# Selective scan on one core: residual added by TensorE, x1 copied by ScalarE, nine products on GpSimd, fourth step size in chunk 4

## What is computed

```python
x = x + s6(layernorm(x))                      # x1
def s6(x):
    xp = einsum('bld,ed->ble', x, x_proj_w)   # 64 ranks, 16 B, 16 C
    delta = softplus(einsum('blr,dr->bld', xp[..., :64], dt_proj_w) + dt_proj_b)
    deltaA = exp(einsum('bld,dn->bldn', delta, A))
    deltaB_u = einsum('bld,bln,bld->bldn', delta, B, x)
    h = deltaA[t] * h + deltaB_u[t]           # over the 1024 rows, for each (d, n)
    y = einsum('bdn,bn->bd', h, C[t])
    return y + x * D
x = x + chosen_tokens(layernorm(x))           # router, attention, MLP
```

## Time and profile before

| | |
|---|---|
| time, median of 3 runs | 4675.12 us (4675.03 to 4675.64) |
| the profiled execution's own time | 4677.7 us |
| its span in the profile | 4675.8 us |
| busy share of the span: DVE, POOL, PE, ACT | 83%, 76%, 59%, 59% |
| scan stage, about | 75 to 3640 us |
| chosen tokens, about | 3640 to 4676 us |

### The profile page before, as it was taken

How to read it: one execution, slowest core, us unless ns; L and a number is a source line. 1 busy time by engine, 2 the same in 40 slices (tenths; PEclk the granted TensorE clock), 3 DMA queues, 4 the chain that set the end, 5 groups by cost and what they waited for, 6 DMA issues and landing times. The chain is left out here.

```text
span 4675.8 us, 57243 instructions
## 1 busy us (share of the span) xinstructions
PE 2747.1 (59%) x15526; PEld 1014.5 (22%) x15526; DVE 3888.9 (83%) x3306; ACT 2753.9 (59%) x4103; POOL 3546.3 (76%) x1796
## 2 busy tenths in 40 slices
PE   3555454546454546454555545454644179999997
PEld 1111111111111111111111111111111145555553
DVE  3999999999999999999999999999999654445552
ACT  5676767767667676776767676776764322223221
POOL 4999999999999999999999999999998100000000
PEclk7556565656565656565555656565655589999999
DMA  4354545363545445454545454545353300000000
GB/s 102 95 132 113 137 110 152 93 160 84 157 99 148 111 132 134 113 137 108 136 110 132 113 137 109 151 95 159 84 141 69 153 16 21 18 23 18 18 18 7
DMA packets 198208, 472.72 MB, mean 101 GB/s; under 512 B 60688, under 2 KB 61200, under 8 KB 197088
## 3 DMA queue, kind: packets, MB, share of 16 engines
q1 hardware_dynamic: 177136, 452.11, 38.1%
q0 software_dynamic: 20736, 16.88, 1.4%
HBM read 126.83 MB, written 73.43 MB: 43 GB/s over the span
## 5 line engine op out<-in xcount | busy, mean ns | idle before, releaser
L879 POOL TENSOR_TENSOR ch<-hid,cmat 128x1024 f32<-128x1024 f32 x1024 | 2391.4, 2363 | 100.7 <-DVE hid L733 83.8
L733 DVE TENSOR_TENSOR_SCAN hid<-decay,inp 128x1024 f32<-128x1024 f32 x1024 | 2288.2, 2271 | 96.5 <-ACT decay L600 95.2
L600 ACT ACTIVATE decay<-delr,a_neg 128x1024 f32<-128x1024 f32 x1024 | 1136.4, 1112 | 807.4 <-DVE hid L733 797.3
L399 PE MATMUL ps_y<-ch,nsum 128*32 128x256 f32 x8192 | 997.7, 587 | 861.5 <-POOL ch L879 857.0
L722 DVE TENSOR_TENSOR inp<-dx,bmat 128x1024 f32<-128x1024 f32 x832 | 958.4, 1209 | 63.0 <-ACT dx L608 63.0
L399 PEld LDWEIGHTS ps_y<-ch,nsum 128*32 128x32 f32 x8192 | 249.2, 143 | 1597.1 <-POOL ch L879 1369.5
L408 PE MATMUL ps_y<-ident,ysb 128*128 128x128 f32 x512 | 169.4, 432 | 677.2 <-ACT ysb L615 660.6
L844 POOL TENSOR_TENSOR inp<-dxr,bmat 128x1024 f32<-128x1024 f32 x192 | 454.6, 2368 | 0.0
L394 PE MATMUL ps_y<-xhT,dskip 128*32 128x256 f32 x2048 | 272.2, 624 | 143.0 <-DVE xr L743 143.0
L1132 POOL DMA_INDIRECT out_rows<-row,idx_out x16 | 41.2, 2573 | 401.9 <-issue 220.9
L408 PEld LDWEIGHTS ps_y<-ident,ysb 128*128 128x128 f32 x512 | 71.7, 197 | 905.3 <-ACT ysb L615 861.7
(11 more groups left out here) (165 smaller groups left out, 3825.1 us busy)
## 6 DMA issues: line engine op xcount, KB each, us to landing
dxr<-dxT SPq DMA_DIRECT2D x1024, 128.0 KB, 2.4
delr<-delT SPq DMA_DIRECT2D x1024, 128.0 KB, 2.4
xr<-in_x SPq DMA_DIRECT2D x32, 1024.0 KB, 5.5
bmat<-b_and_c SPq DMA_DIRECT2D x256, 128.0 KB, 3.4
cmat<-b_and_c SPq DMA_DIRECT2D x256, 128.0 KB, 2.9
x_rows<-xr SPq DMA_DIRECT2D x16, 2048.0 KB, 7.7
out_rows<-xr SPq DMA_DIRECT2D x32, 1024.0 KB, 4.4
w<-in_w SPq DMA_DIRECT2D x2, 4096.0 KB, 23.8
```

Of the source, the lines that this page charges most:

```text
L399: last = pe.matmul(ps_y[q * CH:(q + 1) * CH, 0:2 * P], nsum[:], ch[:, g, q * 2 * P:(q + 1) * 2 * P], start=False, stop=(g == GROUPS - 1))
L600: nc.scalar.activation(decay[:, g % 2, :], delr[:, c % 2, :], ACT.Exp, scale=a_neg[:, i:i + 1])\
L733: nc.vector.tensor_tensor_scan(hid[:, g, :], decay[:, g % 2, :], inp[:, g, :], 0.0, ALU.mult, ALU.add).then_inc(hid_ready, 1)
L879: nc.gpsimd.tensor_tensor(ch[:, g, :], hid[:, g, :], cmat[:, g, :], ALU.mult).then_inc(ch_ready, 1)
```

## The change

TensorE now adds the residual: after each of the two products that turn y, it adds x itself by a product with the identity, into the same place in PSUM, so that PSUM holds x1. A new `copy_x1` on ScalarE copies that to `xr`, behind the exp of the next chunk's group 0, and it alone now raises `y_added`. VectorE's `add_y` is gone. `OWN_AT` loses chunks 1, 4 and 7, so GpSimd makes nine input products a batch. The fourth step size moves from chunk 1 to chunk 4, its second half on TensorE behind group 1 of that chunk, and its four GpSimd steps to chunks 5 to 7. It therefore comes after the router's use of `aux`, and waits for it. `SUMS1` and `SUMS2` are spread anew over chunks 5 and 6 and over chunks 0 to 2.

```diff
-YADD = 2
-SUMS1 = {(5, 1): range(0, 2), (5, 2): range(2, 4), (5, 3): range(4, 8), (6, 0): range(8, 10), (6, 1): range(10, 12), (6, 2): range(12, 14), (6, 3): range(14, 17)}
+SUMS1 = {(5, 2): range(0, 2), (5, 3): range(2, 5), (6, 0): range(5, 8), (6, 1): range(8, 11), (6, 2): range(11, 14), (6, 3): range(14, 17)}
-SUMS2 = {(0, 1): range(0, 2), (0, 2): range(2, 4), (0, 3): range(4, 8), (1, 0): range(8, 10), (1, 1): range(10, 12), (1, 2): range(12, 14), (1, 3): range(14, 17)}
+SUMS2 = {(0, 2): range(0, 3), (0, 3): range(3, 6), (1, 0): range(6, 8), (1, 1): range(8, 11), (1, 2): range(11, 13), (1, 3): range(13, 15), (2, 0): range(15, 17)}
-Z3 = 1
+Z3 = 4
-         (3, 2): (0, 3, 0), (4, 0): (0, 3, 1), (4, 2): (0, 3, 2), (5, 0): (0, 3, 3)}
+         (5, 2): (0, 3, 0), (6, 0): (0, 3, 1), (6, 2): (0, 3, 2), (7, 1): (0, 3, 3)}
-OWN_AT = (1, 3, 4, 5, 6, 7, 8, 9, 10, 11, 12, 13)
+OWN_AT = (3, 5, 6, 8, 9, 10, 11, 12, 13)
...
             def turn_xhat(b, t):
-                if t == 0 and has(b, 2):
-                    pe.wait_ge(router_sum, b * TC - TC)
...
             def step_size(b, k, h):
+                if k == 3 and h == 0 and has(b, 1):
+                    pe.wait_ge(router_sum, b * TC)
...
-            def turn_y(b, c):
+            def turn_y(b, par, c):
                 pe.wait_ge(ysb_ready, b * CHUNKS + c + 1)
                 for t in range(2):
-                    last = pe.transpose(ps_y[:, (2 + t) * P:(3 + t) * P], ysb[:, t * P:(t + 1) * P], ident[:])
+                    out_t = ps_y[:, (2 + t) * P:(3 + t) * P]
+                    x_t = xr[:, par, :, c * CH:(c + 1) * CH].rearrange("p (q t) d -> p t q d", t=2)[:, t]
+                    pe.matmul(out_t, ysb[:, t * P:(t + 1) * P], ident[:], start=True, stop=False)
+                    last = pe.matmul(out_t.rearrange("p (q d) -> p q d", q=4), ident[:], x_t, start=False, stop=True)
                 last.then_inc(yt_ready, 1)
...
+                        for h, at in ((0, (Z3 - 1, 3)), (1, (Z3, 1))):
+                            if (c, g) == at:
+                                step_size(b, 3, h)
                         for h, at in ((0, (-1, 3)), (1, (0, 0))):
-                            if (c, g) == (Z3 + at[0], at[1]):
-                                step_size(b, 3, h)
...
-            def copy_rw(b):
+            def copy_rw(b, emptied):
+                act.wait_ge(aux_emptied, emptied)
                 nc.scalar.activation(aux[:], rw[:], ACT.Copy).then_inc(rw_ready, 1)
...
+            def copy_x1(b, par, c):
+                act.wait_ge(yt_ready, b * CHUNKS + c + 1)
+                if c == 0:
+                    act.wait_ge(xh_ready, b * TC + TC)
+                nc.scalar.activation(xr[:, par, :, c * CH:(c + 1) * CH].rearrange("p (q t) d -> p t q d", t=2),
+                                     ps_y[:, 2 * P:4 * P].rearrange("p (t q d) -> p t q d", t=2, q=4),
+                                     ACT.Copy).then_inc(y_added, 1)
...
                     for g in (0, 1):
                         if not (final and c == CHUNKS - 1):
                             exp_decay(*nxt, g)
+                        if g == 0 and c > 0:
+                            copy_x1(b, par, c - 1)
+                        elif g == 0 and has(b, 1):
+                            copy_x1(b - 1, 1 - par, CHUNKS - 1)
                         beside(b, par, c, 2 + g)
...
                     for g in range(GROUPS):
                         scan(b, c, g)
-                        if g == YADD:
-                            if c >= 1:
-                                add_y(b, par, c - 1)
-                            elif has(b, 1):
-                                add_y(b - 1, other, CHUNKS - 1)
```

More of the change, by code:

```diff
@@ L424, in body @@
                     if c > 0:
-                        turn_y(b, c - 1)
+                        turn_y(b, par, c - 1)
                     elif has(b, 1):
-                        turn_y(b - 1, CHUNKS - 1)
+                        turn_y(b - 1, 1 - par, CHUNKS - 1)
                     for g in range(GROUPS):
                         sum_states(b, par, c, g)
+                        for h, at in ((0, (Z3 - 1, 3)), (1, (Z3, 1))):
+                            if (c, g) == at:
+                                step_size(b, 3, h)
                         for h, at in ((0, (-1, 3)), (1, (0, 0))):
-                            if (c, g) == (Z3 + at[0], at[1]):
-                                step_size(b, 3, h)
                             for k in range(3):
@@ L447, in _ @@
             batches(pe, body)
-            turn_y(nb_run - 1, CHUNKS - 1)
+            turn_y(nb_run - 1, 1, CHUNKS - 1)
             pe.wait_ge(wcol_ready, nb_run)
@@ L653, in beside @@
                 if has(b, 1):
-                    if at == RW_COPY:
-                        copy_rw(b - 1)
                     if at in SUMS2:
                         ln2_sums(b - 1, 1 - par, SUMS2[at])
+                    if at == RW_COPY:
+                        copy_rw(b - 1, b * NUSE + USE["z", 2, 1] + 1)
                     for t in range(TC):
@@ L703, in _ @@
             copy_y(last, CHUNKS - 1)
-            copy_rw(last)
+            copy_x1(last, 1, CHUNKS - 1)
+            copy_rw(last, nb_run * NUSE)
             ln2_sums(last, 1, range(17))
@@ L734, in scan @@
                                              0.0, ALU.mult, ALU.add).then_inc(hid_ready, 1)
[L736 to L743, removed]
             def router(b, par, h):
@@ L791, in _ @@
             last = nb_run - 1
-            add_y(last, 1, CHUNKS - 1)
             for h in range(2):
```

## The result

The changed kernel takes **4692.99 us** (median of 6 runs, 4691.49 to 4694.39), the kernel before 4675.38 in the same runs: ratio 1.0038, 95% interval 1.0025 to 1.0051. So it is slower by 17.6 us, 0.38%. The forecast of 4690 us, 0.3% slower, was right in sign and size. The profiled span is 4691.5 us.

What follows compares the result with a forecast made beforehand. The prediction took VectorE's work plus its waits, 211.7 + 11.0 us a batch, to bound the kernel. Its terms summed to +1.15 us a batch, +14 in all: 4690 us, about 0.3% slower, range 4630 to 4735.

Steps and rivals of the forecast that it cites:

- VectorE's own work: Sixteen adds go (-5.9 us) and three products come from GpSimd (+3.4): -2.5 us a batch.
- The 5.3 us ahead of (2, 2): VectorE's wait before that scan, laid to ScalarE's row of work in chunk 1, falls to 0.1: -5.2 us a batch.
- Chunk 12's step size: Its second half stands behind TensorE's later restart; scan (13, 2) waits 3.1 us, 0.5 before: +2.65 a batch.
- Chunk 13: Step size behind the later restart: next chunk's third scan at T + 12.8 against 11.1, +1.65 us a batch.
- Chunk 4: Fourth step size's new place, behind the sums of groups 0 and 1: T + 14.1 against 10.0, +4.15 us a batch.
- Chunk 15: Step size behind the later restart: next third scan at T + 13.1 against 11.1, +2.0 us a batch.
- Chunks 8 and 9: Turn of the normalised rows stands behind the restart; a wait of 1.36 us becomes 2.8: +0.8 in both.
- Chunk 10: Four projection products between restart and ScalarE's copy: scan (11, 2) at T + 11.7 against 10.0, +1.7 us a batch.
- The turn: Turning y by four plain products on TensorE takes 2.0 us, between 1.4 and 2.8, where two transpositions took 0.69.
- The clock rises: Rival: TensorE's clock rises to 2.4 GHz, -9.7 us a batch, 4554 us; chance 0.20, mostly for part of it.
- GpSimd is the bound: Rival: GpSimd sets the batch, so the period falls by its 7.1 us, to 4576 us; chance 0.07.
- The copy later still: Rival: slow turn or strided write on ScalarE moves seven restarts by 0.5 us each, +3.5 a batch, 4739 us; chance 0.13.

Runs made afterwards that it cites:

- e4: The kernel before with nine input products on GpSimd in place of twelve, nothing else; 4704.70 us, ratio 1.0056.
- e3: The changed kernel with the fourth step size back in chunk 1, its waits and the router copy's too; 4773.06 us, ratio 1.0199.
- e12: The kernel before with only the fourth step size moved from chunk 1 to chunk 4, with its waits on aux; 4632.99 us, ratio 0.9906.
- e1: The changed kernel with the second halves of all four step sizes ahead of TensorE's wait for x1; 4565.48 us, ratio 0.976.
- e6: The changed kernel with ScalarE's place 1 work of chunks 4, 12, 13 and 15 behind the copy of x1; 4636.56 us, ratio 0.9912.
- e5: The changed kernel with y turned by two transpositions and the residual x left out; 4690.92 us, ratio 1.0025.
- e11: The changed kernel without its residual part: VectorE adds again and y is turned by two transpositions; 4628.95 us, ratio 0.9898.
- e7: e1 with GpSimd's input product for chunk 8 exchanged for chunk 4's; 4562.29 us, ratio 0.9758.
- e8: e7 with ScalarE's place 1 work of chunks 8 and 9 behind the copy of x1; 4535.04 us, ratio 0.9701.
- e14: e8 with two chunk 10 projections ahead of TensorE's wait for x1, two behind group 0, and a tenth GpSimd product; 4545.25 us, ratio 0.9719.

## Why the prediction was right, step by step

- **VectorE's own work**, -2.5 a batch: 211.17 to 208.58, -2.6. Right.
- **The 5.3 us ahead of (2, 2)**: no wait is left there (0.1 forecast). Right in size; but 1.0 of it was ScalarE waiting for GpSimd (see e4) and not ScalarE's own row of work, as the prediction had it. e3 gets 7.83 when the step goes back, e12 shows 44 us for the move by itself.
- **Chunk 12's step size**, +2.65: the wait ahead of (13, 2) is 3.16 for 3.1 forecast. **Chunk 13**: 1.62 for 1.65. **Chunk 4**: 4.02 for 4.15. Right, by the way they were reckoned; e1 and e6 show that the restart is the cause.
- **Chunk 15**: forecast 2.0, measured 2.04 at the edge between the two batches of the loop's body (975.59) and 3.42 at the edge of the loop (1199.51). Right inside the body, mis-sized at the loop's edge, by 1.4 as a wait and by 0.8 as a change from the 0.59 before. There ScalarE stands idle 1.25 us between the step size's last pass and the exp, waiting for nothing that the profile shows, and inside the body it does not (the exp at 1421.43 follows at once). The same pause, 1.12 us, stood there in the kernel before and showed on VectorE as 0.59. The prediction read one chunk for both edges and has no term for it. Why ScalarE pauses there is not shown. Before, then after:

```profile
1189.09 2.15 ACT L600 ACTIVATE decay<-delr,a_neg 128x1024 f32<-128x1024 f32 x2 [1.12 <-issue]
```

```profile
1198.18 2.15 ACT L604 ACTIVATE decay<-delr,a_neg 128x1024 f32<-128x1024 f32 x2 [1.25 <-issue]
```

- **Chunks 8 and 9**: +0.8, measured 0.38 and 0.48, together 0.86.
- **Chunk 10**: +1.7, measured 0.93 in this batch and 1.62 in the next. In this one the first two projection products took 2.57 us and not 3.41: the granted clock was 0.50 (1.2 GHz) from 1118 to 1120 us and 1.00 (2.4 GHz) from 1122 to 1124. In the next they took 3.26, and the trace puts the scan's wait down to GpSimd, as in five batches of the stage. Waiting for ch was one of the prediction's signs of being wrong. But the scan begins 1.29 us after the start of its exp (1350.31), just as where a decay is named, so decay and ch came at nearly the same time, and the trace can't tell which of them held it.

```profile
1120.07 2.57 PE L370 MATMUL aux<-xhT,xproj 128*96 128x512 f32 x4
```

```profile
1351.60 4.47 DVE L751 TENSOR_TENSOR_SCAN hid<-decay,inp 128x1024 f32<-128x1024 f32 x2 [1.62 <-POOL ch L882]
```

- **The turn**: taken as 2.0 us, between 1.4 and 2.8, with 0.3 of it a latency for which it named no row. In chunk 4, at 1.2 GHz throughout, the four products (a product is two instructions, one row) take 2.09, from 1035.17 to the end of the row at 1036.62, which is 0.37 more than four starts 0.43 apart; the copy of x1 took 0.38 for 0.36 taken. TensorE there:

```profile
1035.17 0.80 PE L409 MATMUL ps_y<-ident,ysb 128*128 128x128 f32 x2 [5.43 <-ACT ysb L619]
1035.76 0.63 PE L410 MATMUL ps_y<-xr,ident 128*128 128x128 f32 x2
...
1036.62 0.64 PE L410 MATMUL ps_y<-xr,ident 128*128 128x128 f32 x2
```

- **Missed**: chunk 8's scan waits 1.10 us for GpSimd's own product. The prediction counted what GpSimd is spared but not where the fourth step size's GpSimd products go: its last one, at (7, 1), stands with the Newton steps of the statistics (1077.64 to 1079.07) just ahead of the product for chunk 8. No term of the sum stood for it, and it is larger than the whole miss of the sum, below. GpSimd around it:

```profile
1081.35 2.36 POOL L868 TENSOR_TENSOR dxT<-delT,xhT 128x1024 f32<-128x1024 f32 x1
1083.68 4.65 POOL L882 TENSOR_TENSOR ch<-hid,cmat 128x1024 f32<-128x1024 f32 x2
1088.29 2.35 POOL L847 TENSOR_TENSOR inp<-dxr,bmat 128x1024 f32<-128x1024 f32 x1
```

- **The sum**: 223.15 us a batch forecast, 223.56 measured (from 1049.80 to the same scan at 1496.92, two batches), against 222.0 before. That it came within 0.4 us is in part luck: chunk 8's product (+1.1) and the loop's edge (+0.4 as a mean of the two edges) were too low, chunk 10 (-0.4) and the smaller terms (about -0.3) too high. That makes +0.8; the other 0.4 is not placed.

The rivals. *The clock rises*: the granted clock did rise, to 0.62 in the batch from 0.58, and it shortened chunk 10's projections in this batch, but TensorE still ran the step sizes' products at 1.2 GHz (2.07 us at 1146.01). In chunk 12 the turn itself ran with 0.96 granted (1140 to 1142 us); then TensorE stood idle for the copy of x1, and 0.50 was granted from 1142 to 1148. So the products behind this restart ran at the lower clock. With transpositions the granted clock is 0.680 over the run, with plain products 0.697, and the time is the same within 2 us. The Trainium skill, TensorE: Matmul & The Clock Gate, Part 4, says that a transposition does not count as TensorE activity the way a matmul does. The direction agrees, but four products are also more work than two transpositions, so e5 doesn't separate the two, and it is worth nothing here. *GpSimd is the bound*: e4 rules it out. The Trainium skill, Perfetto Trace Analysis, Identifying the Most-Contended Engine, would have one optimize the busiest engine first; GpSimd was the busiest of the batch, e4 took three products from it, and the time rose by 0.56%. The products went to VectorE, so e4 does not test a faster GpSimd; but it shows that the busiest engine did not set the batch here. *The copy later still*: did not occur; the turns looked at took at most 2.1 us and the write 0.36 to 0.39.

What stays open: why ScalarE pauses at the loop's edge, the 0.4 us of the sum that no term holds, and the part of e3's extra 23 us beyond GpSimd's late products. None was tried by itself.

## What to carry to other kernels

When the release of an in-order engine moves to another engine, list what stands behind that wait on its queue, and who needs it: here 6.1 us less work and 2.4 us less waiting for y on VectorE (e11 against the changed kernel, a mean of two batches) were paid with some 13 us of new waits a batch. Work that doesn't need the awaited thing belongs ahead of the wait; with the second halves of the step sizes alone ahead of it the same change ran 2.4% faster than before, not 0.38% slower, though that reordering, in the kernel before, was worth nothing. With two projections ahead too, and with e7's and e8's moves, it ran 3.55% faster. Judge the parts of a bundled change apart: here the step's move was worth -44 us and the residual part +64.

## What was not expected of the hardware

A plain fp32 product of 128 columns costs what was worked out from the long ones: starts are 0.43 us apart at 1.2 GHz (1035.76 and 1036.62 are two products apart) and 0.22 to 0.23 at 2.4 GHz (1141.06, 1141.29, 1141.51 in chunk 12), and the one that reads x in strided rows costs no more than the one that turns y. ScalarE's write of 128x256 to strided rows of x took 0.38 us, against 0.36 for its write to contiguous ones. And GpSimd's lateness was a matter of place in e7: busy for 208.6 of a batch's 223.9 us, it held VectorE up by 1.1 us with the product for chunk 8, and with the same number of products in other places it did not. In e14, where one product behind another held VectorE up by 3.65 us, amount and place changed together.
